# Attention inner loop regrouped from one head and two key blocks to one key block and two heads, with two PSUM evictions moved from VectorE to ScalarE

## The chip, the cores and the metric

The kernel runs on the 8 cores of one Trainium2 chip. The batch of 16 sequences is split over the cores, two sequences of 2048 tokens to each; the cores run the same program and exchange nothing. The metric is the device time of the slowest core in microseconds (us), lower is better.

## The reference

Each sequence (2048 tokens by 1024 channels) goes through layer norm, then through two branches whose product is added to the input:

```python
xn = _layernorm(x)
# attention: 16 heads of 64; keys and values from a strided depthwise convolution of xn
q = xn @ q_w.T + q_b                       # 2048 queries
xd = conv1d(xn, conv_w, stride=2, kernel 3) + conv_b
k = xd @ k_w.T + k_b ; v = xd @ v_w.T + v_b    # 1024 keys
att = softmax(einsum('bhnd,bhmd->bhnm', q, k) * scale)
s = einsum('bhnm,bhmd->bhnd', att, v) @ out_w.T + out_b
# eight experts, each over all tokens (hidden 2048), summed, times a gate factor per token
h = gelu(einsum('nd,edh->neh', xn, w1) + b1) ; y = einsum('neh,ehd->ned', h, w2) + b2
g = silu((y * norm_g).sum(experts))
out = x + s * g
```

## The kernel before

One function, `build_program`, calls `emit(engine, fn, reads, writes)` for every instruction group. `emit` works out the semaphore waits from the buffers named, and at the end each engine gets its groups **in the order in which they were emitted**. Nothing reorders them: the order of the Python loops is the order of each engine's queue. Within one group on TensorE (several matmuls in one `fn`) the waits stand ahead of the first matmul and the signal behind the last.

The work for each of the two sequences of a core is: layer norm and gate per 128 tokens (L345 to L381), convolution and the key and value projections (L425, L431), then two halves of 1024 tokens. Each half runs the eight experts (first layer L479 with its Gelu at L486, second layer L508 accumulated into `yb` at L529, Silu at L539), and then attention in two groups of 512 queries (`qt`). So there are 2 x 2 x 2 = 8 attention stages in the span.

One attention stage:

- Query projection: 8 groups of 8 matmuls (L563) into `pF` and `pE` in turn; VectorE adds the bias and writes `qt_sb` (L569).
- For each of 8 head pairs `pr2`, for each of 4 pairs of key blocks `kp`: four score matmuls (L583 for the even head on array rows 0 to 63, L587 for the odd head on rows 64 to 127). The even head's two key blocks fill the two halves of `pSC0` (1024 columns), the odd head's fill `pSC1`. They are one group: it waits until both buffers are free. ScalarE then takes the exponential of `pSC0` (L595) and of `pSC1` (L599) into `Xt[0]` and `Xt[1]`. TensorE multiplies with the values: two matmuls of the even head into `pC` (L607, L611), which wait for `Xt[0]`, and two of the odd head into `pD` (the same lines), which wait for `Xt[1]`. Row 64 of `pC` and `pD` collects the sum of the exponentials.
- At the end of a head pair: ScalarE takes Ln and Exp of the two sums (L619, L623, each twice), two one-row matmuls spread the reciprocals over the partitions into `pE` (L628, L630), VectorE copies `pE` into `RB` (L635) and scales `pC` and `pD` into `attn_o` (L638, L642). The next head pair's first value matmul waits for that, since it writes `pC`.
- Output projection of the 512 queries (L653, L656), the product with `yb` (L663), and a DMA that accumulates into the output (L669).

TensorE's queue in the loop over `kp` is thus: 4 score matmuls, 2 value matmuls of the even head, 2 of the odd head, 4 score matmuls of the next `kp`.

Of the kernel before, what the change touches and what calls it, by code (L numbers as in the profile page):

```python
# [10 lines left out]
AF = mybir.ActivationFunctionType  # L11
ALU = mybir.AluOpType
# [8 lines left out]
SCALE_ATT = 0.125  # L21
# [11 lines left out]
def build_program(seq=2048, bpc=2, debug=False):  # L33
    NT = seq // 128
    NK = seq // 2
    NKB = NK // 128
# [39 lines left out]
    with ExitStack() as es:  # L76
# [5 lines left out]
        kf = sb("kf", [128, 8, NK], BF16)  # L82
        vpx = sb("vpx", [128, NKB, 1040], BF16)
# [5 lines left out]
        qt_sb = sb("qt", [128, 8, 512], BF16)  # L89
        Xt = [sb(f"Xt{i}", [128, 1024], BF16) for i in range(2)]  # L90
        attn_o = sb("attn_o", [128, 8, 512], BF16)
        RB = [sb(f"RB{i}", [128, 512], F32) for i in range(2)]
# [11 lines left out]
        qb = sb("qbs", [128, 8], F32)  # L104
# [43 lines left out]
        def emit(eng, fn, reads=(), writes=(), extra=()):  # L148
            waits = []
            for b in reads:  # L150
                if b.w is not None:
                    waits.append(b.w)
            for b in writes:
                if b.w is not None:
                    waits.append(b.w)
                waits.extend(b.rs)
            waits.extend(e for e in extra if e is not None)
            if eng in dma_sems:
                sem = dma_sems[eng][dma_idx[eng] % 2]
                dma_idx[eng] += 1  # L160
                if cnt[id(sem)] > 0:
                    waits.append((sem, cnt[id(sem)]))
                cnt[id(sem)] += 16
            else:
                sem = eng_sem[eng]
                cnt[id(sem)] += 1
            ev = (sem, cnt[id(sem)])
            items.append((eng, waits, fn, sem, ev[1]))
            for b in reads:
                b.rs.append(ev)  # L170
            for b in writes:
                b.w = ev
                b.rs = []
            return ev
# [113 lines left out]
        for b in range(bpc):  # L288
# [165 lines left out]
            for Hh in range(NHALF):  # L454
# [103 lines left out]
                for qt in range(NCH):  # L558
                    q0 = ht0 + qt * 512
                    for oc in range(8):  # L560
                        pb, pbuf = [(pF, bpF), (pE, bpE)][oc % 2]
                        emit('tensor', (lambda oc, q0, pb: lambda e: [
                                e.matmul(pb[:, :],  # L563
                                         W1H[:, cc, oc * 128:(oc + 1) * 128],
                                         xn[:, cc, q0:q0 + 512],
                                         start=(cc == 0), stop=(cc == 7))
                                for cc in range(8)][-1])(oc, q0, pb),
                             reads=[bW1, bXN], writes=[pbuf])
                        emit('vector', (lambda oc, pb: lambda e: e.tensor_scalar(  # L569
                                out=qt_sb[:, oc, :], in0=pb[:, :],  # L570
                                scalar1=qb[:, oc:oc + 1], scalar2=None,
                                op0=ALU.add))(oc, pb),
                             reads=[pbuf, bQB], writes=[bQT[oc]])

                    NKP = NKB // 2
                    for pr2 in range(8):
                        for kp in range(NKP):
                            def scm(e, pr2=pr2, kp=kp):
                                last = None
                                for half in range(2):  # L580
                                    kcc = 2 * kp + half
                                    col = slice(half * 512, half * 512 + 512)
                                    e.matmul(pSC0[:, col],  # L583
                                             kf[0:64, pr2, kcc * 128:(kcc + 1) * 128],
                                             qt_sb[0:64, pr2, :],
                                             start=True, stop=True)
                                    last = e.matmul(  # L587
                                        pSC1[:, col],
                                        kf[64:128, pr2, kcc * 128:(kcc + 1) * 128],
                                        qt_sb[64:128, pr2, :],  # L590
                                        start=True, stop=True)
                                return last
                            emit('tensor', scm, reads=[bKF, bQT[pr2]],
                                 writes=[bS0a, bS0b, bS1a, bS1b])
                            emit('scalar', (lambda kp: lambda e: e.activation(  # L595
                                    out=Xt[0][:, :], in_=pSC0[:, :], func=AF.Exp,
                                    scale=SCALE_ATT))(kp),
                                 reads=[bS0a, bS0b], writes=[bXt[0]])
                            emit('scalar', (lambda kp: lambda e: e.activation(  # L599
                                    out=Xt[1][:, :], in_=pSC1[:, :], func=AF.Exp,  # L600
                                    scale=SCALE_ATT))(kp),
                                 reads=[bS1a, bS1b], writes=[bXt[1]])
                            for hp in range(2):
                                h = 2 * pr2 + hp
                                pav, pavb = [(pC, bpC), (pD, bpD)][hp]
                                def avm(e, h=h, kp=kp, pav=pav, hp=hp):
                                    e.matmul(pav[0:65, :],  # L607
                                             vpx[:, 2 * kp, h * 65:(h + 1) * 65],
                                             Xt[hp][:, 0:512], start=(kp == 0),
                                             stop=False)  # L610
                                    return e.matmul(  # L611
                                        pav[0:65, :],
                                        vpx[:, 2 * kp + 1, h * 65:(h + 1) * 65],
                                        Xt[hp][:, 512:1024],
                                        start=False, stop=(kp == NKP - 1))
                                emit('tensor', avm, reads=[bVPX, bXt[hp]],
                                     writes=[pavb])
                        for hp, (pav, pavb) in enumerate([(pC, bpC), (pD, bpD)]):
                            emit('scalar', (lambda pav: lambda e: e.activation(  # L619
                                    out=rtmp[:, :], in_=pav[64:65, :],  # L620
                                    func=AF.Ln))(pav),
                                 reads=[pavb], writes=[bRT])
                            emit('scalar', (lambda hp: lambda e: e.activation(  # L623
                                    out=recips[0:1, hp * 512:(hp + 1) * 512],
                                    in_=rtmp[:, :], func=AF.Exp, scale=-1.0))(hp),
                                 reads=[bRT], writes=[bREC])
                        def rbm(e):
                            e.matmul(pE[:, :], selA[0:1, :], recips[0:1, 0:512],  # L628
                                     start=True, stop=False)
                            return e.matmul(pE[:, :], selB[0:1, :],  # L630
                                            recips[0:1, 512:1024],
                                            start=False, stop=True)
                        emit('tensor', rbm, reads=[bSelA, bSelB, bREC], writes=[bpE])
                        rbs = pr2 % 2
                        emit('vector', (lambda rbs: lambda e: e.tensor_copy(  # L635
                                out=RB[rbs][:, :], in_=pE[:, :]))(rbs),
                             reads=[bpE], writes=[bRB[rbs]])
                        emit('vector', (lambda pr2, rbs: lambda e: e.tensor_tensor(  # L638
                                out=attn_o[0:64, pr2, :], in0=pC[0:64, :],
                                in1=RB[rbs][0:64, :], op=ALU.mult))(pr2, rbs),  # L640
                             reads=[bpC, bRB[rbs]], writes=[bAO])
                        emit('vector', (lambda pr2, rbs: lambda e: e.tensor_tensor(  # L642
                                out=attn_o[64:128, pr2, :], in0=pD[0:64, :],
                                in1=RB[rbs][64:128, :], op=ALU.mult))(pr2, rbs),
                             reads=[bpD, bRB[rbs]], writes=[bAO])
# [128 lines left out]
```

How the kernel before makes its waits and increments, by code:

```python
        def body(eng, name):  # L710
            for (e, ws, fn, sem, evv) in items:
                if e != name:
                    continue
                for (s, v) in ws:
                    nv = rank[id(s)][v] * unit[id(s)]
                    key = (name, id(s))
                    if hw.get(key, -1) >= nv:
                        continue
                    hw[key] = nv
                    eng.wait_ge(s, nv)
                ins = fn(eng)
                if ins is not None and sem is not None \
                        and evv in waited.get(id(sem), ()):
                    ins.then_inc(sem, unit[id(sem)])
```

## Time and profile before

| | |
|---|---|
| timed runs | 6245.96 and 6991.68 us, median 6618.82 |
| profiled execution | 6244.91 us; span of its slowest core (core 1) 6243.3 us, cores 6215.4 to 6243.3 |
| TensorE busy | 5035.4 us (81%) |
| ScalarE busy | 1619.6 us (26%) |
| VectorE busy | 1112.3 us (18%) |
| mean granted TensorE clock | 0.882 of full |

The expert stages fill most of the span at a granted clock of 1.00; the attention stages are the four places in the 40 slices of the page where the digit of PE falls to 6 or 7 and that of PEclk to 5 or 6. In the first eight or nine slices (to about 1300 us) the DMA engines are mostly busy: a pass rewrites the weights to bf16 in DRAM through SBUF, beside the layer norm and the first expert stage.

How to read the rows: times are us from the span's start or ns where marked; a timeline row gives start, duration, engine, line, operation and operands, the number of instructions merged, and in brackets how long the engine had been idle before it and what released it. PE is TensorE, ACT ScalarE, DVE VectorE. Ends of matmuls are modelled; starts are recorded.

### The profile page before, as it was taken

How to read it: one execution, taken by the hardware profiler on the slowest of the kernel's cores; microseconds unless marked ns; L12 is line 12 of the kernel's file. 1: busy time of each engine (PE TensorE's matmuls, PEld its weight loads, DVE VectorE, ACT ScalarE, POOL GpSimd, SP SyncE). 2: the span in 40 equal slices, each digit the busy share in tenths (PEclk: the TensorE clock that was granted, in tenths of full speed). 3: DMA queues.
4: the chain of work that ended last, by engine and by line, in shares of the span. 5: the costliest groups of instructions: out<-in, count | busy, mean ns of one | idle time of the engine just before them, and what ended most of it. 6: DMA issues, size and time to landing. Idle time of an engine off the chain costs nothing.

```text
span 6243.3 us, 62270 instructions; the slowest of 8 cores (6215.4 to 6243.3 us)
## 1 busy us (share of the span) xinstructions
PE 5035.4 (81%) x21220; PEld 1927.0 (31%) x21220; DVE 1112.3 (18%) x1746; ACT 1619.6 (26%) x2517; POOL 177.3 (3%) x218
## 2 busy tenths in 40 slices
PE   1199999995689999996632999999866999999766
PEld 0033334341124444431111344444211344444211
DVE  2211111121111111111123111111111111111111
ACT  4111111125321111134433111111334111111433
POOL 1010111000000000000000000000000000000000
PEclk9999999995689999995655999999865999999765
DMA  8998889720122112120011222121110222222100
GB/s 184 176 204 197 198 193 217 169 81 0 27 54 67 69 68 68 68 75 2 12 41 48 68 68 72 64 76 60 54 27 1 81 68 68 68 68 73 36 14 14
DMA packets 240173, 499.18 MB, mean 80 GB/s; under 512 B 8020, under 2 KB 49108, under 8 KB 239620
## 3 DMA queue, kind: packets, MB, share of 16 engines
q1 hardware_dynamic: 151268, 327.32, 16.7%
q0 software_dynamic: 88608, 167.87, 14.1%
q8 instruction: 189, 3.10, 0.2%
q14 instruction: 108, 0.88, 0.1%
HBM read 478.45 MB, written 109.07 MB: 94 GB/s over the span
## 4 chain that ended last, share of the span: by engine, by line
PE 72%; DMA 9%; ACT 9%; issue 4%; DVE 4%; another core or an unknown queue 2%; ACTq 0%; POOL 0%; DVEq 0%; POOLq 0%; SPq 0%
PE pSC L479 27%; PE pC L508 14%; PE pD L508 14%; PE pSC L583 3%; ACT Xt L595 3%; PE pC L607 2%; PE pC L611 1%; PE pD L607 1%; DMA out<-sg 1%; DMA W1H<-w1b 1%; DMA qt<-w 1%; ACT regA L486 1%; ACT recips L623 1%; PE pD L515 1%
## 5 line engine op out<-in xcount | busy, mean ns | idle before, releaser
L479 PE MATMUL pSC<-xn,W1H 128*128 128x512 bf16 x8192 | 1797.7, 380 | 18.8 <-DMA W1H<-w1b 14.6
L486 ACT ACTIVATE regA<-pSC,b1Ts 128x512 bf16<-128x512 f32 x1024 | 703.7, 687 | 3103.0 <-PE pSC L479 3102.2
L508 PE MATMUL pC<-W2H,regA 128*128 128x512 bf16 x4096 | 973.5, 381 | 166.8 <-ACT regA L486 147.9
L479 PEld LDWEIGHTS pSC<-xn,W1H 128*128 128x128 bf16 x8192 | 796.8, 98 | 993.2 <-issue 48.8
L508 PE MATMUL pD<-W2H,regA 128*128 128x512 bf16 x4096 | 971.5, 380 | 0.0
L529 DVE SCALAR_TENSOR_TENSOR yb<-pC,yb 128x512 f32<-128x512 f32 x480 | 332.0, 692 | 2465.0 <-PE pC L515 1363.0
L508 PEld LDWEIGHTS pC<-W2H,regA 128*128 128x128 bf16 x4096 | 376.6, 98 | 680.6 <-issue 274.1
L508 PEld LDWEIGHTS pD<-W2H,regA 128*128 128x128 bf16 x4096 | 380.1, 98 | 482.6 <-issue 60.7
L595 ACT ACTIVATE Xt<-pSC 128x1024 bf16<-128x1024 f32 x256 | 262.2, 1024 | 740.1 <-PE pSC L587 740.0
L607 PE MATMUL pC<-Xt,vpx 128*65 128x512 bf16 x256 | 146.5, 572 | 374.7 <-ACT Xt L595 291.0
L529 DVE SCALAR_TENSOR_TENSOR yb<-pD,yb 128x512 f32<-128x512 f32 x480 | 332.0, 692 | 610.7 <-PE pD L515 360.8
L377 PE MATMUL pSC<-identS,xntm 128*128 128x128 bf16 x256 | 64.0, 266 | 297.0 <-DVE xntm L369 261.1
L599 ACT ACTIVATE Xt<-pSC 128x1024 bf16<-128x1024 f32 x256 | 260.5, 1018 | 0.0
L587 PE MATMUL pSC<-qt,kf 64*128 64x512 bf16 x512 | 252.0, 592 | 0.0
L583 PE MATMUL pSC<-qt,kf 64*128 64x512 bf16 x512 | 251.5, 590 | 0.0
L635 DVE COPY RB<-pE 128x512 f32<-128x512 f32 x64 | 44.3, 692 | 1156.2 <-PE pE L630 1156.2
L607 PEld LDWEIGHTS pC<-Xt,vpx 128*65 128x65 bf16 x256 | 32.5, 127 | 587.4 <-issue 587.4
L669 POOL DMA_DIRECT2D out<-sg x64 | 54.3, 848 | 4968.0 <-DVE sg L663 4965.6
L607 PE MATMUL pD<-Xt,vpx 128*65 128x512 bf16 x256 | 146.7, 573 | 12.9 <-ACT Xt L599 12.5
L611 PE MATMUL pD<-Xt,vpx 128*65 128x512 bf16 x256 | 152.3, 595 | 0.0
L611 PE MATMUL pC<-Xt,vpx 128*65 128x512 bf16 x256 | 152.1, 594 | 0.0
L628 PE MATMUL pE<-recips,selA 1*128 1x512 bf16 x64 | 36.9, 576 | 131.6 <-ACT recips L623 131.6
(125 smaller groups left out, 2059.4 us busy)
## 6 DMA issues: line engine op xcount, KB each, us to landing
W1H<-w1b SPq DMA_DIRECT2D x64, 2048.0 KB
W2H<-w2b SPq DMA_DIRECT2D x64, 2048.0 KB
attn_o<-w POOLq DMA_DIRECT2D x32, 1024.0 KB, 13.7
qt<-w POOLq DMA_DIRECT2D x32, 1024.0 KB, 13.7
xt<-x SPq DMA_DIRECT2D x32, 512.0 KB
w1b<-attn_o POOLq DMA_DIRECT2D x16, 1024.0 KB, 6.0
w1b<-qt POOLq DMA_DIRECT2D x16, 1024.0 KB, 5.9
w2b<-attn_o POOLq DMA_DIRECT2D x16, 1024.0 KB, 5.9
```

The lines of the kernel that those rows point to most:

```text
L377: emit('tensor', (lambda s, cc, pslot: lambda e: e.transpose(pslot, xn_tm[s][:, cc * 128:(cc + 1) * 128], identS[:, :]))(s, cc, pslot), re ...
L479: e.matmul(ph, W1H[:, cc, uc * 128:(uc + 1) * 128], xn[:, cc, t0:t0 + 512], start=(cc == 0), stop=(cc == 7))
L486: lambda e: e.activation(out=regA[:, uc, tsub * 512:(tsub + 1) * 512], in_=ph, func=AF.Gelu, bias=b1T[:, uh * 8 + uc, e_i:e_i + 1])
L508: last = e.matmul(py[:, :], regA[:, uc, c0:c0 + 128], W2H[:, uc, ocn * 512:(ocn + 1) * 512], start=(uc == 0), stop=(uc == 7 and uh == 0))
L515: last = e.matmul(py[:, :], onesB[0:1, :], rowA[0:1, ocn * 512:(ocn + 1) * 512], start=False, stop=True)
L529: return e.scalar_tensor_tensor(out=yb[:, tg, ocn * 512:(ocn + 1) * 512], in0=py[:, :], scalar=1.0, in1=yb[:, tg, ocn * 512:(ocn + 1) * 51 ...
L583: e.matmul(pSC0[:, col], kf[0:64, pr2, kcc * 128:(kcc + 1) * 128], qt_sb[0:64, pr2, :], start=True, stop=True)
L587: last = e.matmul(pSC1[:, col], kf[64:128, pr2, kcc * 128:(kcc + 1) * 128], qt_sb[64:128, pr2, :], start=True, stop=True)
L595: emit('scalar', (lambda kp: lambda e: e.activation(out=Xt[0][:, :], in_=pSC0[:, :], func=AF.Exp, scale=SCALE_ATT))(kp), reads=[bS0a, bS0b ...
L599: emit('scalar', (lambda kp: lambda e: e.activation(out=Xt[1][:, :], in_=pSC1[:, :], func=AF.Exp, scale=SCALE_ATT))(kp), reads=[bS1a, bS1b ...
L607: e.matmul(pav[0:65, :], vpx[:, 2 * kp, h * 65:(h + 1) * 65], Xt[hp][:, 0:512], start=(kp == 0), stop=False)
L611: return e.matmul(pav[0:65, :], vpx[:, 2 * kp + 1, h * 65:(h + 1) * 65], Xt[hp][:, 512:1024], start=False, stop=(kp == NKP - 1))
```

## The change

It edits only the attention stage.

1. The loop over `kp` (4 steps, 2 key blocks each) becomes a loop over `kc` (8 steps, 1 key block each). A step's score group is two matmuls, even head into columns 0 to 511 and odd head into columns 512 to 1023 of one buffer, `pSC0` for even `kc` and `pSC1` for odd. One exponential of 128x1024 per step goes to `Xt[kc % 2]`. One value group of two matmuls, even head into `pC` and odd head into `pD`, follows it; it writes both and so waits for both.
2. The bias addition of the query projection moves from VectorE to ScalarE (Identity with bias).
3. The copy of `pE` into `RB` moves from VectorE to ScalarE (Identity).

The diff, cut to its core:

```diff
-                        emit('vector', (lambda oc, pb: lambda e: e.tensor_scalar(
-                                out=qt_sb[:, oc, :], in0=pb[:, :],
-                                scalar1=qb[:, oc:oc + 1], scalar2=None,
-                                op0=ALU.add))(oc, pb),
+                        emit('scalar', (lambda oc, pb: lambda e: e.activation(
+                                out=qt_sb[:, oc, :], in_=pb[:, :], func=AF.Identity,
+                                bias=qb[:, oc:oc + 1]))(oc, pb),
                              reads=[pbuf, bQB], writes=[bQT[oc]])
...
-                        for kp in range(NKP):
-                            def scm(e, pr2=pr2, kp=kp):
-                                for half in range(2):
-                                    kcc = 2 * kp + half
-                                    col = slice(half * 512, half * 512 + 512)
-                                    e.matmul(pSC0[:, col], kf[0:64, pr2, kcc...], qt_sb[0:64, pr2, :], ...)
-                                    last = e.matmul(pSC1[:, col], kf[64:128, pr2, kcc...], qt_sb[64:128, pr2, :], ...)
-                            emit('tensor', scm, reads=[bKF, bQT[pr2]],
-                                 writes=[bS0a, bS0b, bS1a, bS1b])
-                            emit('scalar', Exp pSC0 -> Xt[0]) ; emit('scalar', Exp pSC1 -> Xt[1])
-                            for hp in range(2):
-                                def avm(...): 2 matmuls, key blocks 2*kp and 2*kp+1, into pC or pD
-                                emit('tensor', avm, reads=[bVPX, bXt[hp]], writes=[pavb])
+                        for kc in range(NKB):
+                            pset, pb1, pb2 = [(pSC0, bS0a, bS0b),
+                                              (pSC1, bS1a, bS1b)][kc % 2]
+                            def scm(e, pr2=pr2, kc=kc, pset=pset):
+                                e.matmul(pset[:, 0:512], kf[0:64, pr2, kc...], qt_sb[0:64, pr2, :], ...)
+                                return e.matmul(pset[:, 512:1024], kf[64:128, pr2, kc...], qt_sb[64:128, pr2, :], ...)
+                            emit('tensor', scm, reads=[bKF, bQT[pr2]], writes=[pb1, pb2])
+                            emit('scalar', Exp pset -> Xt[kc % 2])
+                            def avm(e, h0=h0, h1=h1, kc=kc):
+                                e.matmul(pC[0:65, :], vpx[:, kc, h0...], Xt[kc % 2][:, 0:512], ...)
+                                return e.matmul(pD[0:65, :], vpx[:, kc, h1...], Xt[kc % 2][:, 512:1024], ...)
+                            emit('tensor', avm, reads=[bVPX, bXt[kc % 2]], writes=[bpC, bpD])
...
-                        emit('vector', (lambda rbs: lambda e: e.tensor_copy(
-                                out=RB[rbs][:, :], in_=pE[:, :]))(rbs),
+                        emit('scalar', (lambda rbs: lambda e: e.activation(
+                                out=RB[rbs][:, :], in_=pE[:, :],
+                                func=AF.Identity))(rbs),
                              reads=[bpE], writes=[bRB[rbs]])
```

## Rows read from the trace of the kernel before

**Rows 1.** The page, part 4: share of the span's chain, by engine.

```profile
PE 72%; DMA 9%; ACT 9%; issue 4%; DVE 4%; another core or an unknown queue 2%; ACTq 0%; POOL 0%; DVEq 0%; POOLq 0%; SPq 0%
```

**Rows 2.** Windows, first score to last L628: stretch, length, PE busy, granted clock, DMA, GB/s.

```profile
1406.70:1567.20 160.50, 94.33 (x272) 0.57 0.00 0
...
6050.70:6209.30 158.60, 93.95 (x272) 0.57 0.00 0
```

**Rows 3.** Timeline: one step of two key blocks, granted clock 0.50.

```profile
1511.09 0.60 PE L583 MATMUL pSC<-qt,kf 64*128 64x512 bf16 x1
...
1511.50 0.63 PE L587 MATMUL pSC<-qt,kf 64*128 64x512 bf16 x1
...
1512.28 1.02 ACT L595 ACTIVATE Xt<-pSC 128x1024 bf16<-128x1024 f32 x1 [2.51 <-PE pSC L587]
...
1513.56 0.61 PE L607 MATMUL pC<-Xt,vpx 128*65 128x512 bf16 x1 [1.43 <-ACT Xt L595]
...
1513.96 0.63 PE L611 MATMUL pC<-Xt,vpx 128*65 128x512 bf16 x1
...
1514.88 0.63 PE L611 MATMUL pD<-Xt,vpx 128*65 128x512 bf16 x1
...
1515.44 0.60 PE L583 MATMUL pSC<-qt,kf 64*128 64x512 bf16 x1
```

**Rows 4.** Timeline: the same step, granted clock 1.00.

```profile
1411.49 0.38 PE L587 MATMUL pSC<-qt,kf 64*128 64x512 bf16 x1
...
1412.02 1.02 ACT L595 ACTIVATE Xt<-pSC 128x1024 bf16<-128x1024 f32 x1 [1.43 <-PE pSC L587]
...
1413.30 0.38 PE L607 MATMUL pC<-Xt,vpx 128*65 128x512 bf16 x1 [1.44 <-ACT Xt L595]
...
1413.52 0.38 PE L611 MATMUL pC<-Xt,vpx 128*65 128x512 bf16 x1
...
1414.42 0.38 PE L611 MATMUL pD<-Xt,vpx 128*65 128x512 bf16 x1
...
1414.73 0.39 PE L583 MATMUL pSC<-qt,kf 64*128 64x512 bf16 x1
```

**Rows 5.** Timeline: from one head pair to the next, granted clock 0.50.

```profile
1502.18 0.63 PE L611 MATMUL pC<-Xt,vpx 128*65 128x512 bf16 x1
...
1502.90 0.59 ACT L619 ACTIVATE rtmp<-pC 1x512 f32<-1x512 f32 x1 [0.47 <-PE pC L611]
...
1503.09 0.63 PE L611 MATMUL pD<-Xt,vpx 128*65 128x512 bf16 x1
...
1505.76 0.58 PE L628 MATMUL pE<-recips,selA 1*128 1x512 bf16 x1 [2.04 <-ACT recips L623]
...
1506.70 0.60 PE L583 MATMUL pSC<-qt,kf 64*128 64x512 bf16 x1
...
1506.88 0.69 DVE L635 COPY RB<-pE 128x512 f32<-128x512 f32 x1 [18.34 <-PE pE L630]
...
1508.46 0.68 DVE L642 TENSOR_TENSOR attn_o<-pD,RB 64x512 bf16<-64x512 f32 x1
...
1509.25 0.61 PE L607 MATMUL pC<-Xt,vpx 128*65 128x512 bf16 x1 [1.51 <-DVE attn_o L642]
```

**Rows 6.** Windows over the first attention stage, columns as in rows 2.

```profile
1406.70:1418.00 11.30, 4.93 (x25) 1.00 0.01 1
1418.00:1567.20 149.20, 89.40 (x249) 0.54 0.00 0
```

**Rows 7.** Groups by line of ScalarE: busy us, mean ns, idle before.

```profile
L381 ACT ACTIVATE xn<-pSC 128x128 bf16<-128x128 bf16 x256 | 71.1, 278 | 80.3 <-PE pSC L377 67.7 <-ACT xn L381 0.7
...
L431 ACT ACTIVATE kf<-pF,kbs 128x512 bf16<-128x512 f32 x16 | 11.0, 687 | 149.2 <-PE pF L425 149.2
...
L595 ACT ACT_TABLE_LOAD x4 | 5.1, 1283 | 51.1 <-PE pSC L587 51.1
L348 ACT ACT_TABLE_LOAD x1 | 1.3, 1283 | 14.5 <-DVE lnst L345 14.5
```

More of the change, by code:

```diff
@@ L573, in build_program @@
                              reads=[pbuf, bQB], writes=[bQT[oc]])
-                    NKP = NKB // 2
                     for pr2 in range(8):
-                        for kp in range(NKP):
-                            def scm(e, pr2=pr2, kp=kp):
-                                last = None
-                                for half in range(2):
-                                    kcc = 2 * kp + half
-                                    col = slice(half * 512, half * 512 + 512)
[L583 to L592, printed above, removed]
-                            emit('tensor', scm, reads=[bKF, bQT[pr2]],
-                                 writes=[bS0a, bS0b, bS1a, bS1b])
[L595 to L602, printed above, removed]
-                            for hp in range(2):
[L604 to L617, printed above, removed]
@@ new lines, in build_program @@
+                        h0, h1 = 2 * pr2, 2 * pr2 + 1
+                        for kc in range(NKB):
+                            pset, pb1, pb2 = [(pSC0, bS0a, bS0b),
+                                              (pSC1, bS1a, bS1b)][kc % 2]
+                            def scm(e, pr2=pr2, kc=kc, pset=pset):
+                                e.matmul(pset[:, 0:512],
+                                         kf[0:64, pr2, kc * 128:(kc + 1) * 128],
+                                         qt_sb[0:64, pr2, :],
+                                         start=True, stop=True)
+                                return e.matmul(
+                                    pset[:, 512:1024],
+                                    kf[64:128, pr2, kc * 128:(kc + 1) * 128],
+                                    qt_sb[64:128, pr2, :],
+                                    start=True, stop=True)
+                            emit('tensor', scm, reads=[bKF, bQT[pr2]],
+                                 writes=[pb1, pb2])
+                            emit('scalar', (lambda kc, pset: lambda e: e.activation(
+                                    out=Xt[kc % 2][:, :], in_=pset[:, :],
+                                    func=AF.Exp, scale=SCALE_ATT))(kc, pset),
+                                 reads=[pb1, pb2], writes=[bXt[kc % 2]])
+                            def avm(e, h0=h0, h1=h1, kc=kc):
+                                e.matmul(pC[0:65, :],
+                                         vpx[:, kc, h0 * 65:(h0 + 1) * 65],
+                                         Xt[kc % 2][:, 0:512], start=(kc == 0),
+                                         stop=(kc == NKB - 1))
+                                return e.matmul(pD[0:65, :],
+                                                vpx[:, kc, h1 * 65:(h1 + 1) * 65],
+                                                Xt[kc % 2][:, 512:1024],
+                                                start=(kc == 0),
+                                                stop=(kc == NKB - 1))
+                            emit('tensor', avm, reads=[bVPX, bXt[kc % 2]],
+                                 writes=[bpC, bpD])
```

## The prediction

> **What bounds the kernel now.** Read the chain that ended last first: three quarters of it is TensorE, most of that the expert matmuls, which the change does not touch [rows 1]. The change lives in eight attention stages. The windows from the first score matmul to the last reciprocal matmul (L628) of each give their lengths, 160.5 us in the first and 158.6 us in the last; all eight add up to 1282.1 us, and their granted clock is 0.52 to 0.58, so mostly the lower level, 1.2 GHz [rows 2]. Then read the timeline of one step. It repeats every 4.35 us (1511.09 to 1515.44) and no engine is full in it: four score matmuls, then TensorE waits 1.43 us until the first exponential is done, its two value matmuls run while the second exponential does, then the second head's two, then the next scores [rows 3]. The step is a chain that passes from TensorE to ScalarE and back once per two key blocks. The second exponential is partly hidden behind the first head's value matmuls; that is all the overlap there is. So what counts is how often the chain is handed over, and what runs during the handover.
>
> **The loop over key blocks.** The sum of busy work is kept: the same matmuls, and 8 exponentials of 128x1024 per head pair as before. What changes is TensorE's queue. It becomes S(0), A(0), S(1), A(1), ... (S the score pair, A the value pair), and A(kc) waits for the exponential of S(kc). S(kc+1) writes the other PSUM buffer and needs nothing from A(kc), but it is queued behind it. So while ScalarE works on kc, TensorE holds at A(kc) and S(kc+1) holds with it; and ScalarE has nothing to do while A(kc) and S(kc+1) run. The two score buffers alternate, but are never in use at once. That the queue really holds back ready work can be seen at the change of head pair: the next scores need neither the reciprocals nor a busy buffer, yet they start at 1506.70, behind L628, for which TensorE had waited 2.04 us [rows 5].
>
> The period of one key block, from starts at 1.2 GHz [rows 3]: last score pair to exponential 0.78 (1511.50 to 1512.28); exponential to first value matmul 1.28 (1512.28 to 1513.56, of which 1.02 is the instruction); first to second value matmul 0.40; last value matmul to next score 0.56 (1514.88 to 1515.44). Sum 3.02, so 6.04 us for two key blocks instead of 4.35. At 2.4 GHz the same four starts give 0.53 + 1.28 + 0.22 + 0.31 = 2.34 us [rows 4].
>
> **The change of head pair.** Before, Ln of the even head's sum started 0.19 us before the odd head's last matmul even did (1502.90 against 1503.09) [rows 5]; after, both heads finish with the same group, so it starts behind the end of that last matmul: 0.63 for the matmul plus 0.09 for the signal (1502.18 + 0.63 to 1502.90, the same handover for the even head), 0.72. From Ln to L628 2.86 us (1502.90 to 1505.76), from there to the next score 0.94 [rows 5].
>
> The RB copy: VectorE 0.69 [rows 5] against 0.687 for a 128x512 Identity from PSUM on ScalarE [rows 7], so equal. VectorE started it 0.18 us after the next score pair's start; ScalarE would end it at 0.87 and is free for the first exponential then, whose scores are ready at 0.78: cost about 0.1. The first value pair must now wait for both scalings on VectorE: copy end 0.87, 0.1 handover, two multiplications 0.79 apart and 0.68 long, 0.11 to TensorE (L642 from 1508.46, 0.68 long, and L607 at 1509.25), 2.55 us after the first score. The exponential alone would allow 0.8 + 1.28 = 2.08, so VectorE sets it, by 0.47 us.
>
> One head pair at 1.2 GHz, from first score: first value matmul 2.55, second 2.95, second score pair 3.51, eighth 3.51 + 6 x 3.02 = 21.63, last value matmul + 0.78 + 1.28 + 0.40 = 24.09, Ln + 0.72 = 24.81, L628 + 2.86 = 27.67, next score + 0.94 = 28.61. A stage is 7 x 28.61 + 27.67 = 227.9 us. The same sum at 2.4 GHz (0.38 for the matmul, 0.22 and 0.31 for the pitches, those of [rows 4] for L628 to the next score too): 2.55, 2.77, 3.08, 17.12, 19.15, Ln at 19.62, L628 at 22.48, next score at 23.01; a stage 183.6 us.
>
> **The clock.** In the first stage the clock was 1.00 for the first 11.3 us, carried over from the dense query projection, and 0.54 on average after it [rows 6]. TensorE was busy 89.40 of 149.20 us in that second part, 60%, and the grant fell nevertheless. After the change the same matmuls are spread over 40% more time, so I expect the same start and no recovery behind it: 11.3 us at full clock do the work of 11.3 x 3.02 / 2.34 = 14.6 us, which takes 3.3 us off: 224.6. Four stages follow a Silu and begin with a table load of 1.28 us on the chain [rows 7], 0.64 per stage on average: 225.2. No recovery at all or the same share as before moves a stage by plus 3.3 or minus 3.
>
> **The query bias on ScalarE.** 8 instructions per stage, 0.69 each [rows 7], every 1.7 us of TensorE's projection, on an engine that is idle there. I cost it at nothing; the cover is the 8 matmuls of 0.22. The last one ends near the first scores and could hold the first exponential by 0.2 us, 2 us in all. If it pulls the table load forward, up to 5.1 us come back (4 loads, [rows 7]). I take neither.
>
> **The sum.** 8 x 225.2 = 1802 against 1282.1: plus 520 us, of which the loop is about 64 x 4 x 1.69 = 433 and the head-pair boundary and the lost clock the rest. On the profiled execution's 6244.9 us (span 6243.3) that is 6765 us. The shown runs are 6246 and 6992 with median 6619; the profiled one agrees with the lower, and the forecast is for executions like it. From 2% on, 125 us, a difference counts as one.
>
> **Rival A, the lock-step at full clock.** If TensorE held 2.4 GHz, 8 x (183.6 + 0.64) = 1474, plus 192: 6437 us. For it: the grant did come back for short stretches, 0.54 being above 0.50 [rows 6]. Against it: a busy share of 60% lost it, and the new step is thinner. Half the time at full clock would give 6600. Chance 0.10.
>
> **Rival B, the buffers do overlap (the other side).** If S(kc+1) ran while ScalarE works on kc, the step would be bound by TensorE's own pitches, 0.40 + 0.56 + 0.40 = 1.36 us at 1.2 GHz [rows 3]; a head pair 2.55 + 7 x 1.36 + 0.40 + 0.72 + 2.86 + 0.94 = 17.0 us against 20.2 now (first stage, 160.5 us and 0.94 for the missing step to a next score, over 8), 64 x -3.2 = -205: 6040 us. It decides from one point: whether a score pair starts between an exponential's start and the value matmul that waits for it. Against it stands the held-back score of [rows 5]. Chance 0.03. The Trainium skill, "Perfetto Trace Analysis", section Matmuls, speaks for this rival: independent matmul groups should rotate through PSUM banks so that the eviction of one overlaps the next group's matmuls. By that rule the new rotation of two score buffers would give the 6040 us of this rival. "TensorE: Matmul & The Clock Gate", section Part 2, says that only weight loads are pulled ahead and matmuls stay in program order; the trace agrees (start 1506.70 behind 1505.76), and by this rule the rival falls and the sum stays 6765.
>
> **Rival C, a table switch at each head pair.** If Identity needed another table than Ln and Exp, each RB copy would bring two loads of 1.28: 64 x 2.57 = 164 more, 6930 us. Against it: 256 Identity evictions of the layer norm stand among Ln and Exp, and its lines carry a single load, the first [rows 7]. Chance 0.03.
>
> **Rival D, the handovers cost less than read,** so that the time stays within 2%. A head pair could then grow by no more than 125 / 64 = 1.95 us; with a 1.02 us exponential alone on the chain eight times that is out of reach unless half the handovers vanish. Chance 0.03.
>
> **Chances.** The forecast case 0.81, with its own range 6700 to 6830: all at 1.2 GHz gives 8 x (227.9 + 0.64), 6791, and 0.07 us more on each of 512 key blocks 6827; the same clock share as before 6740 or less. The range of 8 in 10 reaches part of the way to rival A: 6650 to 6840. Faster 0.03, within 2% 0.03, slower 0.94.
>
> **What would show it.** Right: a steady score-to-score pitch of 3.0 us per key block with TensorE idle about 1.4 us before each value pair; head pairs 28.6 us apart; stages near 225 us; granted clock 0.50 to 0.54 in them; expert stages unchanged. Wrong: a score between exponential and value matmul (rival B), a clock near 1.00 (A), table loads at the RB copy (C). If the first value matmul of a head pair starts 2.1 us after the score instead of 2.55, the VectorE term is mis-sized, by 30 us in all.

## The result, and the profile after

The changed kernel is slower: 1.0865 times the kernel before, 95% interval 1.0837 to 1.0893. Its profiled execution has a span of 6775.4 us on the slowest core (core 6), against 6243.3 us before. Executions of either kernel scatter widely (before 6238 to 6992 us, changed 6755 to 7575 us), so the ratio and all comparisons below use the undisturbed ones: about 6240 us before, about 6780 us after.

Of the page of the kernel after, the line of part 1 (busy us, share of the span, instructions) and the granted clock in 40 slices:

```profile
PE 5126.6 (76%) x21220; PEld 1948.9 (29%) x21220; DVE 1020.3 (15%) x1618; ACT 1722.8 (25%) x2645; POOL 177.3 (3%) x218
...
PEclk9999999966589999966556999999565999999565
```

The work is the same (21220 matmuls before and after), yet the span grew by 532 us. The windows from the first score matmul to the last L617 (L628 before) of each attention stage say where, with the columns of [rows 2]; the first and the last of the eight:

```profile
1403.20:1631.40 228.20, 107.03 (x272) 0.51 0.00 0
...
6514.30:6741.00 226.70, 106.86 (x271) 0.51 0.00 0
```

The eight lengths add up to 1821.0 us against 1282.1: plus 538.9. The stretches between the stages (layer norm, experts, query and output projections) add up to 4954.4 us against 4961.2. So all of the loss is in the attention inner loop; the rest of the span is 7 us shorter. The granted clock of the eight stages, 0.52 to 0.58 before, is 0.51 in each of them after.

The timeline after, one key block and the start of the next, against [rows 3]:

```profile
1504.63 0.60 PE L584 MATMUL pSC<-qt,kf 64*128 64x512 bf16 x1
1505.39 1.02 ACT L591 ACTIVATE Xt<-pSC 128x1024 bf16<-128x1024 f32 x1 [1.98 <-PE pSC L584]
...
1506.67 0.61 PE L596 MATMUL pC<-Xt,vpx 128*65 128x512 bf16 x1 [1.43 <-ACT Xt L591]
...
1507.07 0.63 PE L600 MATMUL pD<-Xt,vpx 128*65 128x512 bf16 x1
...
1507.63 0.61 PE L580 MATMUL pSC<-qt,kf 64*128 64x512 bf16 x1
```

Read it as a relay. Scores at 1504.63, exponential at 1505.39, value matmuls at 1506.67 and 1507.07, next scores at 1507.63: 3.00 us, and at no moment do both engines work. The bracket of the exponential says ScalarE was idle 1.98 us before it, the bracket of the value matmul that TensorE was idle 1.43 us. Before, TensorE had the same 1.43 us once per **two** key blocks [rows 3]; now it has it at each.

The change of head pair after, against [rows 5]:

```profile
1513.08 0.63 PE L600 MATMUL pD<-Xt,vpx 128*65 128x512 bf16 x1
1513.81 0.59 ACT L608 ACTIVATE rtmp<-pC 1x512 f32<-1x512 f32 x1 [1.38 <-PE pD L600]
...
1516.67 0.58 PE L617 MATMUL pE<-recips,selA 1*128 1x512 bf16 x1 [2.95 <-ACT recips L612]
...
1517.61 0.60 PE L580 MATMUL pSC<-qt,kf 64*128 64x512 bf16 x1
...
1517.88 0.60 ACT L624 ACTIVATE RB<-pE 128x512 f32<-128x512 f32 x1 [1.36 <-PE pE L619]
1518.37 1.02 ACT L591 ACTIVATE Xt<-pSC 128x1024 bf16<-128x1024 f32 x1
...
1519.43 0.68 DVE L632 TENSOR_TENSOR attn_o<-pD,RB 64x512 bf16<-64x512 f32 x1
...
1520.27 0.61 PE L596 MATMUL pC<-Xt,vpx 128*65 128x512 bf16 x1 [2.05 <-DVE attn_o L632]
```

Ln now starts 0.73 us behind the start of the last value matmul (before, 0.19 us ahead of it), and the first value matmul of the next pair starts 2.66 us behind its scores, released by the second scaling (L632).

### The profile page after: what moved, and what is told of

It is laid out like the page before. It is cut to its first block, busy times and chain, and to the rows that moved or that the text cites. A ratio compares the mean times of both kernels' runs of the same rounds, so it can differ in the third digit from the quotient of the medians.

```text
span 6775.4 us, 62460 instructions; the slowest of 8 cores (6744.6 to 6775.4 us)
## 1 busy us (share of the span) xinstructions
PE 5126.6 (76%) x21220; PEld 1948.9 (29%) x21220; DVE 1020.3 (15%) x1618; ACT 1722.8 (25%) x2645; POOL 177.3 (3%) x218
## 4 chain that ended last, share of the span: by engine, by line
PE 72%; ACT 14%; issue 6%; DVE 4%; DMA 3%; another core or an unknown queue 2%; ACTq 1%; DVEq 0%; POOLq 0%; SPq 0%
PE pSC L479 25%; PE pC L508 14%; PE pD L508 13%; ACT Xt L591 7%; PE pC L596 5%; PE pSC L580 4%; PE pD L600 3%; ACT regA L486 1%; DMA W2H<-w2b 1%; PE pC L515 1%; ACT recips L612 1%; PE pD L515 1%; DMA out<-sg 1%; ACT rtmp L608 1%
## 5 line engine op out<-in xcount | busy, mean ns | idle before, releaser
L596 PEld LDWEIGHTS pC<-Xt,vpx 128*65 128x65 bf16 x512 | 66.8, 131 | 1014.8 <-issue 1014.8
L628 DVE TENSOR_TENSOR attn_o<-pC,RB 64x512 bf16<-64x512 f32 x64 | 43.7, 682 | 1857.1 <-ACT RB L624 1857.1
L600 PE MATMUL pD<-Xt,vpx 128*65 128x512 bf16 x512 | 322.6, 630 | 0.0
L580 PE MATMUL pSC<-qt,kf 64*128 64x512 bf16 x512 | 306.5, 599 | 0.0
L584 PE MATMUL pSC<-qt,kf 64*128 64x512 bf16 x512 | 306.5, 599 | 0.0
L617 PE MATMUL pE<-recips,selA 1*128 1x512 bf16 x64 | 37.0, 579 | 190.0 <-ACT recips L612 190.0
L580 PEld LDWEIGHTS pSC<-qt,kf 64*128 64x128 bf16 x512 | 51.6, 101 | 407.6 <-issue 407.6
L425 PE MATMUL pF<-regA,W1H 128*128 128x512 bf16 x128 | 33.3, 408 | 135.1 <-DMA W1H<-awb 101.9
L377 PEld LDWEIGHTS pSC<-identS,xntm 128*128 128x128 bf16 x256 | 26.4, 104 | 330.2 <-issue 329.3
```

Of the source, the lines that this page charges most:

```text
L377: emit('tensor', (lambda s, cc, pslot: lambda e: e.transpose(pslot, xn_tm[s][:, cc * 128:(cc + 1) * 128], identS[:, :]))(s, cc, pslot), re ...
L580: e.matmul(pset[:, 0:512], kf[0:64, pr2, kc * 128:(kc + 1) * 128], qt_sb[0:64, pr2, :], start=True, stop=True)
L584: return e.matmul(pset[:, 512:1024], kf[64:128, pr2, kc * 128:(kc + 1) * 128], qt_sb[64:128, pr2, :], start=True, stop=True)
L596: e.matmul(pC[0:65, :], vpx[:, kc, h0 * 65:(h0 + 1) * 65], Xt[kc % 2][:, 0:512], start=(kc == 0), stop=(kc == NKB - 1))
L600: return e.matmul(pD[0:65, :], vpx[:, kc, h1 * 65:(h1 + 1) * 65], Xt[kc % 2][:, 512:1024], start=(kc == 0), stop=(kc == NKB - 1))
```

## Experiments

Each ran beside the kernel before on the same chip, and a ratio is to that. Where none is given the times are compared; the kernel before took 6244 us on that chip. Line numbers in the rows are those of the kernel at hand.

**The loop alone.** The changed kernel with both evictions back on VectorE.

```diff
-emit('scalar', activation(out=qt_sb[:, oc, :], in_=pb, func=Identity, bias=qb[...]))
+emit('vector', tensor_scalar(out=qt_sb[:, oc, :], in0=pb, scalar1=qb[...], op0=add))
-emit('scalar', activation(out=RB[rbs], in_=pE, func=Identity))
+emit('vector', tensor_copy(out=RB[rbs], in_=pE))
```

> The regrouped loop alone; both evictions stay on VectorE. Theory (the loop's lock-step and the later Ln carry everything, the evictions nothing): the time of the changed kernel or 7 us below it, since the RB copy then starts 0.1 us earlier per head pair: ratio to before 1.085, head pairs 28.5 us apart. Rival (the evictions on ScalarE hold up the exponentials and carry a good part): clearly below the changed kernel, 6700 us or less, and fewer idle gaps before the exponentials.

Measured: ratio 1.0863 (1.0834 to 1.0892), median 6780 us, against 1.0865 for the whole change. The loop carries all of it. The 7 us that the RB copy might have given back can't be told from nothing at this interval. The trace is finer: with the copy on VectorE the first value matmul of a pair starts 2.59 us behind its scores (1520.29 to 1522.88), with the copy on ScalarE mostly 2.66, and head pairs are 28.57 us apart instead of 28.63 (L618 from 1462.3 to 1633.7 over 6 pairs). That is about 0.06 us per pair, some 3 us in all.

**The evictions alone.** The kernel before with both evictions on ScalarE.

> The two evictions alone move to ScalarE; the loop is that of before. Theory: no more than 7 us (0.1 us on 64 head pairs) over before, ratio 1.000 to 1.002, head pairs 20.5 us apart. Rival (ScalarE is on the chain and gets 0.69 us more per head pair and 5.5 us per projection): 64 x 0.69 + 8 x 5.5 = 88 us more, ratio 1.014.

Measured: ratio 1.0013 (1.0000 to 1.0026), 8 us, near the small value and far from the 88 us of the rival. ScalarE has time to spare there. Where the 8 us lie is open, and the interval reaches down to nothing: in the first attention stage the first value matmul of a pair starts 2.52 us behind its scores at six of the seven changes of head pair, as in the kernel before, and the seventh has 2.60 for 2.55. The ratios of the loop alone and of the evictions alone, 1.0863 and 1.0013, leave nothing for an effect of both together.

**Scores ahead of values.** The changed kernel, same instructions and buffers, another queue order:

```diff
+emit_score(0); emit_exp(0)
 for kc in range(NKB):
-    emit_score(kc); emit_exp(kc)
+    if kc + 1 < NKB:
+        emit_score(kc + 1); emit_exp(kc + 1)
     emit_av(kc)
```

> The changed kernel with the score pair and exponential of key block kc+1 put ahead of the value pair of kc in the queues, within a head pair. Theory (the queue order alone keeps the two score buffers from overlapping): two key blocks are then in flight on the same chain of 3.02 us at 1.2 GHz or 2.34 us at 2.4 GHz, so 1.51 or 1.17 us per key block instead of 3.02; stages of about 144 or 119 us instead of 228; total 6110 us at the lower clock, 5910 at the higher, below the kernel before. Rival (buffers or engines, not the order, limit the step; clock or ScalarE): stays above 6500 us.

Measured: ratio 0.9648 (0.9629 to 0.9667), 6017 to 6029 us. Same matmuls, same exponentials, same two score buffers as the changed kernel, and 750 us less than it. So the buffers, the amount of work and the evictions are excluded as the cause; the order of the queue is shown. The total lies between the two values expected, 6110 us at the lower clock and 5910 at the higher. Its timeline, two consecutive exponentials and the matmuls around them:

```profile
1473.72 0.60 PE L580 MATMUL pSC<-qt,kf 64*128 64x512 bf16 x1
...
1474.32 0.61 PE L600 MATMUL pC<-Xt,vpx 128*65 128x512 bf16 x1
1474.72 0.63 PE L604 MATMUL pD<-Xt,vpx 128*65 128x512 bf16 x1
1474.77 1.02 ACT L594 ACTIVATE Xt<-pSC 128x1024 bf16<-128x1024 f32 x1 [0.79 <-PE pSC L584]
1475.28 0.60 PE L580 MATMUL pSC<-qt,kf 64*128 64x512 bf16 x1
...
1476.05 1.02 ACT L594 ACTIVATE Xt<-pSC 128x1024 bf16<-128x1024 f32 x1 [0.26 <-PE pSC L584]
```

Scores to scores 1.56 us (1473.72 to 1475.28) at the lower clock, instead of 3.00: two key blocks are in flight on the same chain. Scores start at 1475.28 in the middle of the exponential that runs from 1474.77. This is the row that was named beforehand as the mark of overlap, and the changed kernel has none like it. The granted clock of the whole span rose to 0.92, from 0.84 in the changed kernel, and that of the first stage to 0.70 (1404 to 1536 us), from 0.51. So the 750 us are the overlap and a better clock together, both brought by the order alone.

**One value group per head.** The changed kernel with the value pair signalled and waited for head by head:

```diff
-emit('tensor', both matmuls, reads=[bVPX, bXt[kc % 2]], writes=[bpC, bpD])
+emit('tensor', even head,    reads=[bVPX, bXt[kc % 2]], writes=[bpC])
+emit('tensor', odd head,     reads=[bVPX, bXt[kc % 2]], writes=[bpD])
```

> The changed kernel with the value pair split into one group per head, so that each head's accumulator is waited for and signalled alone. Same matmuls, same order. Theory: Ln of the even head starts 0.40 us earlier and the next head pair's even matmul waits for the first scaling alone, so that the odd one sets the chain and another 0.40 us goes: 64 x 0.8 = 51 us less than the changed kernel, about 6725 us. Rival (the boundary term was not on the chain, all the loss is in the steps): no change from the changed kernel.

Measured: ratio 1.0768 (1.0747 to 1.0789), 6724 us median. That is some 55 us below the changed kernel, for 51 expected. In the timeline the even head's value matmul starts while the second scaling still runs, and only the odd head's comes behind it:

```profile
1510.09 0.68 DVE L630 TENSOR_TENSOR attn_o<-pD,RB 64x512 bf16<-64x512 f32 x1
1510.40 0.61 PE L598 MATMUL pC<-Xt,vpx 128*65 128x512 bf16 x1 [1.53 <-ACT Xt L591]
1510.92 0.61 PE L598 MATMUL pD<-Xt,vpx 128*65 128x512 bf16 x1
```

L617's counterpart (L615) comes 27.8 us apart (1424.2 to 1618.8 over 7) instead of 28.6.

**Filling the wait, changed kernel.** Three more 128x512 matmuls per key block into the idle `pF`, between scores and values. They are extra work whose result is not used.

```diff
 emit_score(kc); emit_exp(kc)
+emit('tensor', 3 x matmul(pF, kf[:, 0, 0:128], qt_sb[:, 0, :]), writes=[bpF])
 emit_av(kc)
```

> The changed kernel with three more 128x512 matmuls per key block, whose result is not used, into the idle buffer pF between the score pair and the value pair, where TensorE waits 1.4 us. Theory (the wait is there in any case, and the clock fell because the engine idles): they fit into the wait at either clock and cost nothing; the granted clock in the attention stages rises from 0.5 towards 1.0, the step falls from 3.02 towards 2.34 us, total towards 6440 us, with 0.8 of the way (6510) my guess because TensorE still idles 3 us at each head pair. Rival (the clock does not follow idle time): 6780 us at a clock of 0.50 in the stages.

Measured: 6519 and 6527 us, about 255 us **less** than the changed kernel although each core's TensorE does 1536 matmuls more. Its timeline at the higher level, one key block:

```profile
1507.65 0.39 PE L580 MATMUL pSC<-qt,kf 64*128 64x512 bf16 x1
...
1507.97 0.82 PE L596 MATMUL pF<-qt,kf 128*128 128x512 bf16 x3
1508.19 1.02 ACT L591 ACTIVATE Xt<-pSC 128x1024 bf16<-128x1024 f32 x1 [1.32 <-PE pSC L584]
1509.47 0.38 PE L601 MATMUL pC<-Xt,vpx 128*65 128x512 bf16 x1 [0.68 <-ACT Xt L591]
...
1509.99 0.39 PE L580 MATMUL pSC<-qt,kf 64*128 64x512 bf16 x1
```

The step is 2.34 us (1507.65 to 1509.99), the sum that the prediction had made for 2.4 GHz. TensorE still waits 0.68 us behind the three matmuls, so they lie wholly inside the wait. In windows of 30 us from 1410 to 1560 us the granted clock is 0.82 to 0.84, against 0.50 in the changed kernel. So the clock is a second, real loss, worth at least 255 us of the changed kernel's time, and it comes back when the waits are filled. But the relay is still slower than the kernel before even at this clock (6519 against 6240), and by the sum of rival A it would be at full clock too (6437).

**Filling the wait, kernel before.** The same three matmuls per step of two key blocks.

> The kernel before with three more 128x512 matmuls per step of two key blocks, whose result is not used, into pF in its 1.43 us wait. Theory: clock in the stages rises from 0.56 towards 1.0, the step falls from 4.35 towards 3.47 us, 256 steps x 0.88 = 225 us less, about 6010 to 6050 us in all. Rival (the clock does not follow idle time): 6240 us and 0.56.

> The kernel before with the three unused matmuls in its wait once more, for a comparison on the same chip with undisturbed runs of before. Theory: step 3.47 instead of 4.35 us where the clock is full, 6030 to 6060 us, ratio to before about 0.97. Rival (the clock does not follow idle time): ratio 1.00.

Both runs gave 6048 to 6066 us; the ratio is that of the second, 0.9705 (0.9682 to 0.9727). From 1420 to 1550 us the granted clock is 0.85 to 0.91 in windows of the stage, and the step is 3.47 us at the higher level:

```profile
1505.67 0.39 PE L583 MATMUL pSC<-qt,kf 64*128 64x512 bf16 x1
...
1509.14 0.39 PE L583 MATMUL pSC<-qt,kf 64*128 64x512 bf16 x1
```

That is also the step of the kernel before where its clock was full, without the extra matmuls (1411.26 to 1414.73): they cost nothing, and the gain is the clock. The kernel before was paying 3% for it. Idle time of TensorE costs twice there: for itself, and through the clock of the matmuls between.

The two fill runs also split the loss of the changed kernel. With the waits filled in both, at nearly equal clocks of the whole span (0.94 and 0.955), 6523 us stand against 6057: 466 us remain of the 540. So, as an estimate from these four times, the relay itself carries most of the loss, and the further fall of the clock some 70 us.

**Scores ahead across head pairs,** with the next pair's first exponential behind the four Ln and Exp, once with the evictions on ScalarE and once on VectorE.

```diff
     if kc + 1 < NKB: emit_score(kc + 1); emit_exp(kc + 1)
+    elif pr2 < 7:    emit_score(0, pr2 + 1)
     emit_av(kc)
 ... Ln, Exp, Ln, Exp, reciprocal matmuls
+if pr2 < 7: emit_exp(0)
```

> Scores ahead as in the kernel with scores ahead, and also from one head pair to the next: the next pair's first score pair goes ahead of the last value pair, and its first exponential behind the four Ln and Exp, ahead of the RB copy. Theory: the next pair's first two exponentials run while the reciprocals are spread and scaled, 1.5 to 2 us per change of head pair, 56 changes: 80 to 110 us less than with scores ahead within a pair. Rival (the chain Ln, Exp, L617, RB, scaling sets the boundary whatever runs beside it): 30 us less or nothing.

> The same with both evictions back on VectorE. Now ScalarE is busier than in the changed kernel. Theory: the RB copy no longer stands between two exponentials on ScalarE, 0.6 us of its time per head pair; where ScalarE sets the pace there, 10 to 35 us less than the same kernel with the evictions on ScalarE. Rival (the copy is equally long on either engine and its start set by L619): no difference.

Measured: 6027 to 6031 us, and 6006 to 6030 us, against 6017 to 6029 with scores ahead within a pair only. The 80 to 110 us are not there; the rival of the first holds. For the second, medians of 6015 us against 6027 lean towards the 10 to 35 us expected, but single executions spread over 25 us, so its theory and its rival are left undecided. The timeline of the first of the two tells why nothing came:

```profile
1471.50 0.38 PE L604 MATMUL pD<-Xt,vpx 128*65 128x512 bf16 x1
...
1474.71 1.02 ACT L594 ACTIVATE Xt<-pSC 128x1024 bf16<-128x1024 f32 x1
...
1477.60 0.69 DVE L648 TENSOR_TENSOR attn_o<-pD,RB 64x512 bf16<-64x512 f32 x1
1478.43 0.61 PE L600 MATMUL pC<-Xt,vpx 128*65 128x512 bf16 x1 [2.05 <-DVE attn_o L648]
```

With scores ahead within a pair only, the same place reads:

```profile
1481.40 0.38 PE L604 MATMUL pD<-Xt,vpx 128*65 128x512 bf16 x1
...
1486.44 1.94 ACT L594 ACTIVATE Xt<-pSC 128x1024 bf16<-128x1024 f32 x2
...
1488.33 0.61 PE L600 MATMUL pC<-Xt,vpx 128*65 128x512 bf16 x1 [1.62 <-DVE attn_o L643]
```

The first exponential of the new pair now starts 3.21 us behind the last value matmul, where it was 5.04 us, ends at 1475.73 and then lies waiting: the value matmul starts at 1478.43, when the second scaling is done. From the last value matmul of a pair to the first of the next it is 6.93 us, the same as in the rows above.

**Accumulators copied out.** To test whether the accumulators hold the next pair back, VectorE copies `pC` and `pD` to SBUF at the end of a pair (into the convolution's scratch, idle here), and Ln, Exp, the reciprocal matmuls and the scaling work on the copy, one or two key blocks into the next pair. The value pair is split into one group per head here too, and the next pair's first exponential goes right behind its scores.

```diff
+emit_av: one group per head, writes=[bpC] and writes=[bpD]
+elif pr2 < 7: emit_score(0, pr2 + 1); emit_exp(0)
+for hx, pav in enumerate([pC, pD]):
+    emit('vector', tensor_copy(out=cacc[pr2 % 2][0:65, 512 * hx:...], in_=pav[0:65]))
-Ln, Exp per head; reciprocal matmuls; RB copy; scaling of pC, pD
+after emit_av(0) of the next pair: Ln, Exp of both heads (1x1024 each)
+after emit_av(1): reciprocal matmuls; scaling of the copy, read against pE
```

> Scores ahead, also across head pairs, and at the end of a pair VectorE copies both accumulators (65x512 each) to SBUF, so that the next pair's value matmuls need only wait for those copies; Ln and Exp of both heads are one 1x1024 instruction each, and they, L617's two matmuls and the two scalings run beside the next pair's first steps (the RB copy falls away). Theory (scores ahead across pairs gained nothing because the first value pair waits for the chain Ln, Exp, reciprocal matmuls, RB, scaling through the accumulators): the 7 us from a pair's last value matmul to the next pair's first fall to about 1.5, head pairs from 17.1 to 10.5 to 12.5 us, total 5600 to 5730 us, granted clock in the stages above 0.9. Rival (ScalarE or a third thing paces the boundary): within 50 us of 6025.

Measured: ratio 0.9275 (0.9258 to 0.9291), 5785 us. The boundary:

```profile
1454.48 0.38 PE L602 MATMUL pD<-Xt,vpx 128*65 128x512 bf16 x1
1454.75 0.69 DVE L654 COPY cacc<-pC 65x512 f32<-65x512 f32 x1 [6.11 <-PE pC L602]
...
1455.59 0.38 PE L602 MATMUL pC<-Xt,vpx 128*65 128x512 bf16 x1 [0.40 <-DVE cacc L654]
1456.38 0.38 PE L602 MATMUL pD<-Xt,vpx 128*65 128x512 bf16 x1 [0.41 <-DVE cacc L654]
1456.39 1.05 ACT L611 ACTIVATE cacc<-cacc 1x1024 f32<-1x1024 f32 x1
...
1458.73 0.37 PE L622 MATMUL pE<-recips,selA 1*128 1x512 bf16 x1 [1.11 <-ACT recips L615]
...
1459.30 0.60 PE L580 MATMUL pSC<-qt,kf 64*128 64x512 bf16 x1
```

From last to first value matmul 1.11 us (1454.48 to 1455.59) instead of 6.93, and its bracket names the copy: the accumulators were what held the next pair back, and this is shown. How much of the 240 us below the scores-ahead runs belongs to the copies, and how much to the split value groups, the merged Ln and Exp and the RB copy that fell away, was not taken apart. The total missed its expected range by 55 us. Head pairs are 12.6 us apart (L622, 1421.0 to 1508.9 over 7), just above the 10.5 to 12.5 expected, and the clock in windows of the first stage is 0.74 to 0.88 rather than above 0.9. Ln and Exp of 1.05 us each stand in ScalarE's queue from 1456.39, the reciprocal matmuls wait 1.11 us for them, and the next scores stand behind those: the relay again, once per pair. That this makes the rest of the difference is read from the rows and was not tried. It is the fastest version here, and it beats both kernels.

## Where the prediction was right, and which step failed

**The mechanism** held. The queue S(0), A(0), S(1) with A waiting gives a relay; the summed period of 3.02 us per key block was measured as 3.00; head pairs forecast 28.61 us apart were 28.63 (L617 from 1431.0 to 1631.4 over 7 pairs). The loop-alone and evictions-alone runs give each part the value that the sum had for it, and the order-only run excludes rival explanations that name buffers or engine time.

**The boundary.** Ln's delay, taken as 0.72, is 0.73. The first value matmul, taken as 2.55 us behind the scores, is 2.66 at most changes of head pair (two of the seven in the first stage have 2.55 and 2.62): the copy on ScalarE starts 0.27 us behind the scores, not 0.18 as on VectorE, but takes 0.60 us instead of 0.69 (I had the duration from a bf16 output). The rest are slower handovers than the 0.1 and 0.11 taken: 0.17 from the copy's end at 1518.48 to the first scaling at 1518.65, and 0.16 from the end of the second (1520.11) to the value matmul (1520.27). A term mis-sized by 0.11, some 5 us over the 56 changes of head pair.

**The clock.** I let each stage keep 2.4 GHz for its first 11.3 us, as in [rows 6]. The first 11.8 us after show 0.73:

```profile
1403.20:1415.00 11.80, 4.43 (x15) 0.73 0.00 0
1415.00:1631.40 216.40, 102.60 (x257) 0.50 0.00 0
```

Within it, the clock is down to 0.50 from about 1409 us on. So about half of the credit of 3.3 us was there, and less in the other stages, where the first 11.8 us show 0.63 to 0.70. This is the larger mis-sized term, some 17 us over eight stages (an estimate: 3.3 us times the share of each stage's credit that is missing). The expectation that nothing would recover behind it was right: 0.50. Stages average 227.6 us against 225.2 forecast, 8 x 2.4 = 19 us more; the rest of the span is 7 us shorter. Span 6775.4 against the 6763 or so that the sum implied.

**The query bias** cost about what the prediction named and left out, 2 us in all: the last Identity of a projection holds the first exponential of each stage. In the four stages without a table load that exponential starts 0.75 us behind the scores, against the 0.53 of a step at full clock; in the other four the load starts 0.87 behind them (1403.17 to 1404.04). The table load was not pulled forward. It still stands on the chain behind the last Identity (1404.04, 1.28 us, ahead of the first exponential at 1405.34), so ScalarE's Identity ran without a load after the Silu and the four loads before the exponentials remained.

**The step that failed** is the last one of the sum, its base: the rise of 520 us was put on one execution, the profiled one of 6244.9 us, and handed on as an absolute time, although the prediction itself gave the median of the shown times, 6618.8 us, midway between 6246 and 6992, and said that its forecast was only for executions like the profiled one. Read as it was meant, 6765 us is a rise of 8.3%, where 8.65% was measured (1.0865, 6241 us to 6781). Read against the shown median it is a rise of 2.2%, a quarter of the effect, and the whole range of 6650 to 6840 forecasts only 0.5% to 3.3%. The ratio 1.083 was not stated beside the time; applied to the shown median it would have been 6619 x 1.083 = 7170 us. That 6775 us of the trace lies inside the range therefore says that the mechanism was sized well, and not that the forecast as a change from the shown time was.

**The rivals.** A (full clock): not so by itself (0.51 in the stages), but the fill run shows its price per step to have been well placed, 2.34 us. B (overlap): not so in this order: the first stage of the changed kernel has no score matmul between an exponential's start and the value matmul that waits for it. With the order changed the overlap comes true, with 6027 us for the 6040 worked out, and head pairs 16.9 us apart for 17.0. That the two agree so well is partly luck: the rival put the step at TensorE's own pitches, 1.36 us at the lower clock, and the rows show 1.56 there, while the clock was granted at 0.70 and not 0.50. The rule of the Trainium skill that spoke for it ("Perfetto Trace Analysis", Matmuls: rotate independent groups through PSUM banks so that eviction overlaps matmuls) is borne out by the scores-ahead run and not by the changed kernel: the rotation needs the next group's matmuls to stand ahead of the one that waits. C (table switches): not so, no load at L624. D: not so.

## What to carry to other kernels

Two buffers overlap nothing while the queue of the engine that both fills and empties them alternates "produce k, consume k": put "produce k+1" ahead of the consumer that waits for k, then look for the next buffer that the consumer holds (here the accumulators, through the normalization chain). When regrouping a loop, count the round trips between engines and not the instructions; this regrouping kept every matmul and every exponential and doubled the round trips. And state a forecast as a ratio next to its absolute time, above all when the times shown differ from the execution that it was worked out from.

## What the runs showed of the hardware that I had not expected

Unused matmuls can pay for themselves. The prediction had nothing of it; the expectation of the fill run did (6510 us). 1536 extra 128x512 matmuls per core placed in TensorE's waits made the changed kernel about 255 us faster (6519 and 6527 against about 6780 us), and 768 made the kernel before 3% faster (0.9705), through the granted clock: 0.50 to 0.83 and 0.56 to about 0.9 in the stages, where a 128x512 matmul's pitch is 0.40 us at the lower level and 0.22 at the higher.
